# A four-layer graph network on one core: the seven destination-ordered rounds run from the last edge to the first, with at most two units of rows behind each pair of edge blocks

## The reference, cut to what matters

```python
src = randint(0, 100000, (50000,))
dst = minimum(int(100000 * uniform((50000,)) ** 2.0), 99999)     # then both sorted by dst

# blocks 0 and 1: 2 + 4 rounds of this kind ("sage")
mean = segment_sum(h[src], dst) / maximum(count(dst), 1)
out  = mean @ W_l + b + h @ W_r        # block 0: rows divided by their norm; then relu
# block 2, one round ("gat"): attention grouped by src, values from dst
# block 3, one round ("tr"): q = h[dst] Wq, k = h[src] Wk + e, v = h[src] Wv + e, e = edge_attr @ We
w    = segment_softmax((q * k).sum(-1) / sqrt(128), dst)
out  = segment_sum(v * w, dst) + h @ Wskip + bskip
# each block ends in layernorm(x + block(x))
```

## Time and profile before

| | |
|---|---|
| median of 3 runs | 13957.61 us (13944.32 to 13994.78) |
| the profiled execution's own span | 16848.3 us |
| preparation, up to the first scatter of round 0 | 1751.1 us |
| busy: PE, DVE, POOL, ACT | 8724.5, 7447.1, 7480.4, 4895.5 us |
| mean granted TensorE clock | 0.667 |

### The profile page before, as it was taken

How to read it: one execution, slowest core, us unless ns; L and a number is a source line. 1 busy time by engine, 2 the same in 40 slices (tenths; PEclk the granted TensorE clock), 3 DMA queues, 4 the chain that set the end, 5 groups by cost and what they waited for, 6 DMA issues and landing times. The chain is left out here.

```text
span 16848.3 us, 221135 instructions
## 1 busy us (share of the span) xinstructions
PE 8724.5 (52%) x38799; PEld 6051.7 (36%) x38898; DVE 7447.1 (44%) x21114; ACT 4895.5 (29%) x11500; POOL 7480.4 (44%) x7460
## 2 busy tenths in 40 slices
PE   6654344533344455445545544454544446677765
PEld 2121233422333344334434433343333323344444
DVE  6654234424454122121112113447888864444456
ACT  0000122223444122122212213344555541222257
POOL 2545554354322654554465455433334336554410
PEclk9775566756666566566656766666666667777776
DMA  6000234424443245345424534554333331233367
GB/s 253 1 3 1 75 120 139 156 71 125 135 143 121 87 148 171 94 126 159 152 88 148 171 97 143 169 190 147 120 121 119 120 113 47 79 98 110 118 193 245
DMA packets 1169327, 2072.17 MB, mean 123 GB/s; under 512 B 283810, under 2 KB 292531, under 8 KB 1156371
## 3 DMA queue, kind: packets, MB, share of 16 engines
q1 hardware_dynamic: 662400, 1128.29, 22.2%
q10 hardware_dynamic: 268534, 564.37, 8.7%
q0 software_dynamic: 238336, 378.92, 8.3%
HBM read 1358.91 MB, written 773.68 MB: 127 GB/s over the span
## 5 line engine op out<-in xcount | busy, mean ns | idle before, releaser
L639 POOL DMA_INDIRECT agg<-y_rows,s_idx x3136 | 3246.2, 1035 | 5507.4 <-ACT y_rows L970 2718.8
L883 PE MATMUL o_bank<-b_parts,ones_parts 3*128 3x512 bf16 (+1 forms) x1568 | 786.2, 501 | 3838.8 <-ACT h_t L1043 2893.0
L886 PE MATMUL o_bank<-w_r,h_t 128*128 128x128 f32 x12544 | 2587.7, 370 | 0.0
L1594 DVE TENSOR_TENSOR total<-o_bank,agg_in 128x512 f32<-128x512 f32 (+1 forms) x1568 | 1048.1, 688 | 3377.2 <-DMA agg_in<-agg 2068.9
L886 PEld LDWEIGHTS o_bank<-w_r,h_t 128*128 128x128 f32 x12544 | 2204.2, 264 | 536.9 <-issue 536.2
L1043 ACT ACTIVATE h_t<-ht_bank 128x512 f32<-128x512 f32 (+1 forms) x1568 | 878.3, 594 | 3930.8 <-remote 2694.1
L883 PEld LDWEIGHTS o_bank<-b_parts,ones_parts 3*128 3x128 bf16 (+1 forms) x1568 | 148.9, 95 | 4192.2 <-ACT h_t L1043 3123.9
L970 ACT ACTIVATE y_rows<-edge_bank,inv 128x128 f32<-128x128 f32 x2352 | 658.7, 373 | 2807.7 <-remote 1640.9
L789 PE MATMUL edge_bank<-w_l,run 128*128 128x128 f32 x4704 | 962.0, 383 | 951.7 <-DVE run L1410 776.4
L630 POOL DMA_INDIRECT gath<-node_a,g_idx x1176 | 1124.9, 957 | 513.6 <-issue 355.1
L630 POOL DMA_INDIRECT gath<-node_x,g_idx x784 | 780.1, 995 | 1079.4 <-PE edge_bank L829 646.1
(11 more groups left out here) (257 smaller groups left out, 14785.5 us busy)
## 6 DMA issues: line engine op xcount, KB each, us to landing
agg_in<-agg SPq DMA_DIRECT2D x1560, 256.0 KB
node_a<-h_out ACTq DMA_DIRECT2D x780, 256.0 KB
h_in<-node_a SPq DMA_DIRECT2D x780, 256.0 KB
node_x<-h_out ACTq DMA_DIRECT2D x392, 256.0 KB
node_b<-h_out ACTq DMA_DIRECT2D x392, 256.0 KB
h_in<-node_x SPq DMA_DIRECT2D x390, 256.0 KB
h_in<-node_b SPq DMA_DIRECT2D x390, 256.0 KB
agg<-zeros ACTq DMA_DIRECT2D x96, 1024.0 KB
```

What stands on the lines that cost most here:

```text
L639: pool.indirect_dma_start(agg[order(r)], bass.IndirectOffsetOnAxis(s_idx[q][:, k:k + 1], 0), y_rows[q][:, k, :], None, bounds_check=N - 1, ...
L883: pe.matmul(o_bank[s][0:p, :], ones_parts[:, 0:p], b_parts[:, r, :].unsqueeze(1).to_broadcast([3, RPP, P]), start=True, stop=False, skip_g ...
L886: last = pe.matmul(o_bank[s][0:p, j * P:(j + 1) * P], h_t[s][:, j, 0:p], w_r[r][:], start=False, stop=j == RPP - 1, skip_group_check=True)
L1594: dve.tensor_tensor(flat(total[s], p), o_bank[s][0:p, :], flat(agg_in[s], p), ALU.add).then_inc(sum_ready[s], 1)
```

## The change

In the seven rounds that are ordered by destination everything is walked backwards: edge blocks from the last to the first, the 512 edges of a block reversed, and units from the highest rows down (the rest unit with the very highest rows stays last). The number of units that may have run after pair i is then how many lie above the pair's destinations, and it is also capped at 2i (`most_units`). The gat round keeps its order. Core of the diff:

```diff
+        def block_of(i, q, r):
+            return i * 2 + q if order(r) else i * -2 + (BLOCKS - 1 - q)
+        def table_block(i, q, r):
+            return i * 2 + q if order(r) else i * -2 + (BLOCKS + 1 - q)
-        def group_dram(t, u, s):
+        def group_dram(t, u, s, r):
+            if r < NR and order(r) == 0 and not (isinstance(u, int) and u == UNITS):
+                u = u * -1 + (UNITS - 1)
...
+            pool.iota(most_units[:], pattern=[[2, PAIRS]], base=0, channel_multiplier=0).then_inc(prep_pool, 1)
...
-            dve.tensor_copy(key_f[:], dst_i[:])
-            done(dve.tensor_copy(other_f[:], src_i[:]))
+            dve.tensor_copy(key_f[:], dst_i[:, ::-1])
+            dve.tensor_copy(wt_f[:], scat_f[:, ::-1])
+            done(dve.tensor_copy(other_f[:], src_i[:, ::-1]))
...
-                done(dve.tensor_copy(end, pe_bank[1][0:1, 0:BLOCKS].rearrange("o (i q) -> o i q", q=2)[:, :, 0]))
+                first_keys = pe_bank[1][0:1, 0:BLOCKS].rearrange("o (i q) -> o i q", q=2)
+                done(dve.tensor_copy(end, first_keys[:, :, 0] if t else first_keys[:, ::-1, 1]))
                 done(dve.tensor_scalar(end, end, SHIFT, None, ALU.logical_shift_right))
+                if t == 0:
+                    done(dve.tensor_scalar(end, end, -1.0, float(UNITS - 1), ALU.mult, ALU.add))
+                    done(dve.tensor_scalar(end, end, 0.0, None, ALU.max))
+                    done(dve.tensor_tensor(end, end, most_units[:], ALU.min))
                 done(dve.tensor_scalar(end, end, float(UNITS - 3), None, ALU.min))
...
-                        last = pe.transpose(pe_bank[q][0:EDIM, k * P:(k + 1) * P], attr[q][:, k, :], ident[:])
+                        last = pe.matmul(pe_bank[q][0:EDIM, k * P:(k + 1) * P], attr[q][:, CPB - 1 - k, :], flip[:],
+                                         start=True, stop=True, skip_group_check=True)
```

More of the change, by code:

```diff
@@ L553, in load_h @@
                         sp.sem_inc(sp_turn, 1)
-                        sp.dma_start(flat(h_in[s], width(u, s)), group_dram(h_of, u, s)).then_inc(h_loaded[s], 16)
+                        sp.dma_start(flat(h_in[s], width(u, s)), group_dram(h_of, u, s, r)).then_inc(h_loaded[s], 16)
                 def unit(u, r=r, res_of=res_of):
@@ L559, in unit @@
                         sp.sem_inc(sp_turn, 1)
-                        sp.dma_start(flat(agg_in[s], width(u, s)), group_dram(agg[order(r)], u, s)).then_inc(agg_loaded[s], 16)
+                        sp.dma_start(flat(agg_in[s], width(u, s)), group_dram(agg[order(r)], u, s, r)).then_inc(agg_loaded[s], 16)
                     if res_of is not None:
@@ L564, in unit @@
                             sp.sem_inc(sp_turn, 1)
-                            sp.dma_start(flat(res_in[s], width(u, s)), group_dram(res_of, u, s)).then_inc(res_loaded[s], 16)
+                            sp.dma_start(flat(res_in[s], width(u, s)), group_dram(res_of, u, s, r)).then_inc(res_loaded[s], 16)
                     if not isinstance(u, int) or u + 2 <= UNITS:
@@ L586, in out_unit @@
                     sp.sem_inc(sp_turn, 1)
-                    sp.dma_start(flat(agg_in[s], width(u, s)), group_dram(node_x, u, s)).then_inc(agg_loaded[s], 16)
+                    sp.dma_start(flat(agg_in[s], width(u, s)), group_dram(node_x, u, s, r)).then_inc(agg_loaded[s], 16)
                 if not isinstance(u, int) or u + 2 <= UNITS:
@@ L707, in _ @@
             pe.wait_ge(first_start, 1)
-            pe.transpose(pe_bank[1][0:BLOCKS, 0:1], carry_row[:, 0:BLOCKS], ident[0:1, 0:1]).then_inc(first_start_t, 1)
+            pe.transpose(pe_bank[1][0:BLOCKS, 0:1], carry_row[:, 1:BLOCKS + 1], ident[0:1, 0:1]).then_inc(first_start_t, 1)
             for t in range(2):
@@ L976, in start_marks @@
                     act.wait_ge(shift_ready[q], shift_ready.at(r, i))
-                    act.activation(start_neg[q][:, 0:BLOCK], keep[:, bass.ds((2 * i + q) * BLOCK, BLOCK)], ACT.Copy,
+                    act.activation(start_neg[q][:, 0:BLOCK], keep[:, bass.ds(block_of(i, q, r) * BLOCK, BLOCK)], ACT.Copy,
                                    scale=BIG, bias=-BIG).then_inc(neg_ready[q], 1)
@@ L1035, in store @@
                     act.wait_ge(out_ready[s], out_ready.at(r, u + 1))
-                    act.dma_start(group_dram(h_to, u, s), flat(h_out[s], width(u, s))).then_inc(stored[s], 16)
+                    act.dma_start(group_dram(h_to, u, s, r), flat(h_out[s], width(u, s))).then_inc(stored[s], 16)
                 def front(u, r=r):
@@ L1209, in _ @@
                 dve.memset(unit_end[q][:], 0)
-                dve.memset(idx[q][:, BLOCKS:BLOCKS + 2, :], 0)
-            dve.memset(before_f[:], float(NW + 1))
-            dve.memset(after_f[:], float(NW))
+            dve.memset(idx[0][:, 0:2, :], 0)
+            dve.memset(idx[1][:, BLOCKS:BLOCKS + 2, :], 0)
+            for t in range(2):
+                dve.memset(before_f[t][:], float(NW + 1))
+                dve.memset(after_f[t][:], float(NW))
             dve.memset(all_ones[:], 1.0)
@@ L1305, in _ @@
                     done(dve.tensor_scalar(digit_i[:], src_i[:], LOW_BITS, None, ALU.logical_shift_right))
-                done(dve.tensor_copy(digit_f[:], digit_i[:]))
+                done(dve.tensor_copy(digit_f[:], digit_i[:] if n_pass else digit_i[:, ::-1]))
                 dve.sem_inc(sort_ready, 1)
```

61 lines of the change are left out of this document (34 added, 27 removed).

## The result

| | before | after |
|---|---|---|
| median (range) of 4 runs each | 13976.19 us (13944.32 to 13997.3) | 13323.4 us (13319.57 to 13331.17) |
| ratio, 95% interval | | 0.9533 [0.9517, 0.9549] |

The account below looks back on a forecast made before the run. Each pair was bound by POOL's scatter floor or, with more units, a loop through all engines. Loops -154, end -187, attributes +45, preparation +3 made -293 us (-1.74%): 13715 us from 13957.6, range 13540 to 13920.

Parts of the forecast that it names:

- loops: Seven rounds' pair loops: pair 0 without units, 47 pairs with two each, 11268 us against 11422.0, so -154 us.
- behind the last pair: After each round's last pair: four units left instead of eight, 6.7 us each over seven rounds, uncovered, -187 us.
- attributes: Round 7: four transposes a block become four fp32 matmuls to reverse attributes; half on the path, +45 us (0 to +95).
- preparation: Before the rounds: a few iotas, a copy of 98x512 and three instructions on 49 numbers, +3 us.
- the price of a pair with two units: In the loops: pairs 23 to 29 priced a two-unit pair at 236.1 us, summed over one pair of each round.
- so I take the share and not the difference: Whole kernel: profiled execution 1.207 times the runs' median, so -293 of 16848.3 us was applied as -1.74% to 13957.6 us.
- The form of a pair's cost: In the loops: a pair costs max(floor, c + b x units), with POOL's floor at 20.5 us.
- numbers for successive pairs: Changed trace: scatters of successive pairs 33, 40, 28 to 29, 32 and 46 us apart in rounds 0, 1, 2-4, 5, 7.
- B: Rival: POOL's floor weighs more in the runs than in the profile, loops shrink to about 0.78; -380 us, 13580 us; chance 0.15.
- C: Rival: POOL's floor weighs less in the runs, cost linear in units; no difference that can be told, likely 13990 us; chance 0.15.
- D: Rival: thinly spread units leave TensorE at the low clock, 0.51; slower by 365 us, 14260 us; chance 0.05.
- E: Rival: units run no more evenly, waiting for something other than the table; 13960 to 14000 us; chance 0.03.

Follow-up runs that it names:

- before_two: Unchanged copy of the kernel before, profiled again; it fell on the slower kind of chip: 16841.84 us, beside 16857.19 us.
- after_again: Unchanged copy of the changed kernel, run on the slower kind of chip: 16618.61 us, ratio 0.9855 to the kernel before.
- the three pairs of runs above: Slower kind, each beside the changed kernel: plain transposes with ACT's copy reading backwards, 27 and 7 us less; plain transposes without reversal, 27 us more.
- cap0: Changed kernel with the cap at zero, so all 98 units stand behind the last pair; faster kind: 16668.52 us, ratio 1.1911.
- before_again: Unchanged copy of the kernel before, profiled a second time; it fell on the slower kind of chip: 16815.06 us, beside 16842.44 us.
- before_three: Unchanged copy of the kernel before, profiled on the faster kind of chip: 13978.22 us, beside a median of 13987.34 us.

## Why the forecast fell short

| term | forecast, in us of the 16848.3 | on the faster kind | on the slower (loops, end and preparation: `before_two`, `after_again`, one chip) |
|---|---|---|---|
| loops | -154 | -462.5 | -14 |
| behind the last pair | -187 | -184.4 | -197 |
| attributes | +45 | not measured | +27, +7, -27 (the three pairs of runs above) |
| preparation | +3 | -0.8 | -14 |

**The step that failed is the price of a pair with two units**, "1652.60 us or 236.1 us for one pair of each round", and with it "so I take the share and not the difference". The first was read in an execution on the slower kind; the second spread its excess evenly, which made 128 us of the 154 and 155 of the 187. The excess is not even. Set the two traces of before side by side: a pair with two units 236.1 against 1238.9 / 7 = 177.0 us (1.33 times), the preparation 1751.1 against 1459.2 (1.20), a first pair without units in round 2 22.4 against 20.4 (1.10), a unit behind the last pair 6.7 against 6.6 (1.02), a pair of the gat round 47.1 against 2019.7 / 43 = 47.0 (1.00). The very stretch that the change moves units into had the largest excess. The same working on the rows of the faster kind, first pairs of 20.4 us in six rounds and 32.6 in round 7 (155 us), gives 155 + 47 x 177.0 - 8893.6 = -420 us for the loops and (331.1 - 9.8) / 49 x 28 = -184 behind them: -604 us against the measured -646.9. With the forecast's +45 and +3 that would have been -556 us, or 13420 us: still 97 us above the measured time, 48 of them the terms just added, the rest the loops. So the method stood, and the prices were another chip's.

On the slower kind the total came near the forecast (1.5% on this chip, 1.74% forecast), but in part by luck: the loops gave 14 us and not 154, the attributes took nothing that can be told in place of 45, and the end gave 10 us more. There, evening out gains only about what the four units more in each loop take.

**What held.** The form of a pair's cost; units that are free under POOL's floor; two units for each of 47 pairs, flat along the round; the four units fewer behind the last pair, priced within 3 us before the division by 1.207; preparation, gat round and output pass as they were. Its sign that a two-unit pair costs the same early, mid and late held too (20.4 us in all three windows of round 2, but for pair 47). Its numbers for successive pairs (33, 40, 28 to 29, 32 and 46 us) did not: 21.4, 30.7, 20.4, 22.9 and 40.0, and "no pair at POOL's floor but the first" turned into nearly every pair of rounds 2 to 4.

**The rivals.** B, the floor weighs more in the runs, named the mechanism and its marks (loops shrink, POOL's 1.28 us does not), but ascribed it to the profiling and gave it 0.15. It sized a relu round's gain at 57 us and had nothing for rounds 0 and 1; measured were 72 to 78 in rounds 2 to 4, 93 and 65 in rounds 0 and 1. Its 13580 us was still 257 us above the measured time. For round 0 it missed that two units come within a microsecond of the floor there too (21.3 us in before's pairs). Its objection, that profiling has no reason to spare POOL, was sound, and pointed away from profiling and not from B. C, the floor weighs less, is refuted by the same 1.28 us. D, the clock, is refuted: the mean granted clock rose from 0.701 to 0.733. In round 2 it went from 0.51 to 0.65 in pairs 0 to 5, and from 0.84 to 0.80 in pairs 36 to 47. The Trainium skill ("TensorE: Matmul & The Clock Gate", Why this matters for your kernels) wants TensorE busy without gaps; these rows do not show the loss that this would make here, since spreading the units took little from the dense pairs and gave much to the empty ones. No trace has pairs with two units at a clock of 0.50, so what they would take there stays open; pairs without units take 20.4 us at it (`cap0`). E is refuted by the flat pairs.

**What stays open.** Why the slower chips are slower. The traces show where: hardly in the length of the work (PE is busy 8702.7 us in `before_again` and 8577.5 in `before_three`, at a mean clock of 0.665 and 0.701; DVE, ACT and POOL differ by under 15 us), but between the end of one engine's work and the start of another's. Round 2 of `before_again`, POOL where pair 24 begins, the last gather and the first scatter:

```profile
5997.02 0.95 POOL L630 DMA_INDIRECT gath<-node_x,g_idx  x1 [0.31 <-issue]
6008.01 1.02 POOL L639 DMA_INDIRECT agg<-y_rows,s_idx  x1 [10.04 <-issue]
```

`before_three` where pair 24 begins:

```profile
4813.07 0.94 POOL L630 DMA_INDIRECT gath<-node_x,g_idx  x1 [0.30 <-issue]
4814.32 1.02 POOL L639 DMA_INDIRECT agg<-y_rows,s_idx  x1 [0.30 <-issue]
```

POOL's instructions are equally long (0.94 to 1.02 us); ten microseconds stand ahead of the scatter on one kind and 0.3 on the other. The chain that leads there started late. Ahead of it in `before_again`, TensorE's transposes of a unit, and ScalarE's copy that needs them:

```profile
5983.22 1.04 PE L877 MATMUL ht_bank<-ident,h_in 128*128 128x128 f32 x8
5995.89 0.60 ACT L1043 ACTIVATE h_t<-ht_bank 128x512 f32<-128x512 f32 x1 [14.13 <-remote]
```

The first half of the transposes ends at 5983.82 us, and the update of the semaphore with which it releases ScalarE stands in the trace at 5995.79, 12 us later. In `before_three` the same update stands 13 ns behind the same instruction's end. The profile calls such a releaser "remote", since it finds no instruction that ended just before. The waits of the whole of `before_again` (us in total, times, longest) have many such rows, and among the waits of `before_three` there is none:

```profile
ACT h_t L1043 <- remote: 2786.4, 365, 28.4
ACT y_rows L970 <- remote: 1486.4, 105, 22.6
DVE total L1594 <- remote: 775.7, 155, 16.9
```

Worked out from the semaphore records of the two traces, about 2000 updates of `before_again` stand 1 to 28 us behind the end of the last instruction that could have made them, 1700 of them TensorE's, and 19 of `before_three`, all in the output pass. (Each trace has some 90 more that stand over 100 us behind any such instruction; they aren't counted.) In 95% of the 2000, POOL was in the midst of its indirect DMAs when that instruction ended; of all updates of that trace, 34% fall into such a stretch. The other traces divide in the same way: 2000 to 2200 late updates in each of the 14 of the slower kind, 19 in each of the four of the faster. So the slower kind is the one on which a finished instruction's release can arrive late while POOL issues. What holds the update back was not found, and no run took it away. Nor was the flip's cost measured on the faster kind, where no kernel without it fell.

## What to carry to other kernels

Before a price is taken from a trace, hold the trace's own time against the runs; where they differed by 20% here, no common factor repaired it, and the floor that stayed equal while loops around it stretched was already a sign. Cut the loop by how much moved work each iteration holds, and compare with the floor: work that lies under it is free, so in a round where two units fit under it, even counts win about as much as the uneven ones stuck out (72 us by the table, 78 measured in round 2), and here the direction of the walk was worth nothing. When the part outside the loop is uncovered, a simple count times a measured step prices it well: 184 us against 187, and dividing that by 1.207 made it worse.

## What the runs showed that was not expected

One and the same program, 1.169 million DMA packets in each trace, takes 13944 to 14004 us on the chips of one kind and 16575 to 16904 us on the five that fell to the other, and all runs on one chip stay with its kind. On the slower kind finished instructions release their waiters up to 28 us late, mostly while POOL issues indirect DMAs; on the faster kind that isn't seen outside the output pass. The excess is nil in the gat round (47.0 and 47.1 us a pair), where 180 updates come late too and yet a pair takes no longer, and largest where scatters and gathers are issued back to back beside units. And a change can be worth 4.7% on one kind and 1.5 to 2.2% on the other, because a chain that is shorter than POOL's 16 indirect DMAs on one is longer than them on the other.
